# Layer 1 attention: packed products gathered in bursts every second step, maxima in whole rows over 41 steps a head, quads chained without a drain

## What is computed

```python
qkv = x @ w_qkv + b_qkv
q, k, v = jnp.split(qkv, 3, axis=-1)
q, k, v = (to_heads(q), to_heads(k), to_heads(v))
dots = jnp.einsum('bhid,bhjd->bhij', q, k) * scale
attn = jax.nn.softmax(dots, axis=-1)
out = jnp.einsum('bhij,bhjd->bhid', attn, v)
```

## Time and profile before

| | |
|---|---|
| median of 3 runs | 10340.24 us (10335.65 to 10344.37) |
| span of the profiled execution | 10375.5 us |
| mean granted TensorE clock | 0.809 |
| busy PE, DVE, ACT, GpSimd | 8825.9 (85%), 5783.3 (56%), 4145.5 (40%), 3261.0 us (31%) |
| layer 1 attention | about 3229 to 8560 us of the span |

### The profile page before, as it was taken

How to read it: one execution, slowest core, us unless ns; L and a number is a source line. 1 busy time by engine, 2 the same in 40 slices (tenths; PEclk the granted TensorE clock), 3 DMA queues, 4 the chain that set the end, 5 groups by cost and what they waited for, 6 DMA issues and landing times. The chain is left out here.

```text
span 10375.5 us, 158377 instructions
## 1 busy us (share of the span) xinstructions
PE 8825.9 (85%) x47072; PEld 4663.3 (45%) x47072; DVE 5783.3 (56%) x13683; ACT 4145.5 (40%) x9073; POOL 3261.0 (31%) x1854
## 2 busy tenths in 40 slices
PE   4499989997667999998999989999999885448888
PEld 3355545554444444444444444444444334325555
DVE  4355555555557976675766757766676004324444
ACT  1255555553000055555555555555555660001111
POOL 2000000000000055555555555555555670142211
PEclk8655555555876599999999999999999996569999
DMA  4511121101533001202112021111211004211110
GB/s 137 88 20 20 20 35 20 20 8 49 178 123 103 10 20 28 56 21 56 27 24 56 19 56 30 31 45 30 47 28 41 14 5 127 78 40 42 44 34 21
DMA packets 368839, 480.22 MB, mean 46 GB/s; under 512 B 154040, under 2 KB 322362, under 8 KB 354855
## 3 DMA queue, kind: packets, MB, share of 16 engines
q1 hardware_dynamic: 344551, 426.24, 17.0%
q0 software_dynamic: 23424, 43.45, 1.6%
HBM read 298.80 MB, written 180.34 MB: 46 GB/s over the span
## 5 line engine op out<-in xcount | busy, mean ns | idle before, releaser
L1057 POOL TENSOR_TENSOR a_added<-a_P 128x896 f32<-128x896 f32 x1344 | 2805.3, 2107 | 3517.1 <-ACT a_P L1029 3516.8
L935 DVE TENSOR_REDUCE a_tops<-a_ps 128x1 f32<-128x448 f32 x5600 | 3166.2, 632 | 1322.8 <-PE a_ps L843 1319.5
L1029 ACT ACTIVATE a_P<-a_ps 128x448 f32<-128x448 f32 (+1 forms) x5600 | 2610.3, 548 | 2600.3 <-PE a_ps L901 2599.3
L901 PE MATMUL a_ps<-a_qp,a_kp 98*128 98x448 f32 (+1 forms) x5600 | 1946.8, 399 | 171.4 <-DMA a_qp<-scratch_neg 97.9
L843 PE MATMUL a_ps<-a_hk,a_hq 96*128 96x448 f32 (+1 forms) x4900 | 1922.6, 406 | 118.9 <-DMA a_hk<-scratch_k 96.8
L843 PEld LDWEIGHTS a_ps<-a_hk,a_hq 96*128 96x128 f32 (+1 forms) x4900 | 917.7, 188 | 1205.3 <-DVE a_tops L935 1047.2
L901 PEld LDWEIGHTS a_ps<-a_qp,a_kp 98*128 98x128 f32 (+1 forms) x5600 | 1008.0, 189 | 951.7 <-ACT a_P L1029 637.8
L860 PE MATMUL a_ps<-a_P,a_vt 128*32 128x448 f32 (+1 forms) x11200 | 1362.2, 558 | 0.0
L459 DVE CUSTOM_DVE_ANT_0 n_sm<-n_ps,n_bias 112x448 f32<-112x448 f32 x928 | 578.1, 624 | 850.8 <-PE n_ps L390 850.8
L485 ACT ACTIVATE n_P<-n_sm,n_mx 112x448 f32<-112x448 f32 x928 | 620.2, 668 | 845.4 <-DVE n_mx L459 845.4
L400 PE MATMUL n_ps<-n_idn,n_P 112*112 112x112 f32 x3712 | 923.5, 404 | 21.5 <-DVE n_P L466 21.5
(11 more groups left out here) (174 smaller groups left out, 6476.7 us busy)
## 6 DMA issues: line engine op xcount, KB each, us to landing
a_qp<-scratch_q SPq DMA_DIRECT2D x168, 224.0 KB, 3.8
a_hq<-scratch_q SPq DMA_DIRECT2D x84, 392.0 KB, 7.3
a_hk<-scratch_k SPq DMA_DIRECT2D x84, 392.0 KB, 8.6
a_kp<-scratch_k SPq DMA_DIRECT2D x96, 320.0 KB, 4.9
scratch_t<-o_ts SPq DMA_DIRECT2D x8, 3136.0 KB, 13.2
e_w<-in_w SPq DMA_DIRECT2D x16, 1024.0 KB
p_xs<-in_x SPq DMA_DIRECT2D x4, 3136.0 KB, 15.3
scratch_v<-p_vs SPq DMA_DIRECT2D x4, 3136.0 KB, 12.5
```

What stands on the lines that cost most here:

```text
L901: pe.matmul(PS[0:rows_of(t), i_s % 3, 0:GW], kp[0:98, hh, 128 * t:128 * t + rows_of(t)], qp[0:98, hh, GW * j:GW * j + GW], start=True, sto ...
L935: dve.tensor_reduce(tops[0:rows_of(t), KT * hh + t, k:k + 1], PS[0:rows_of(t), MAX + i % MAXES, 0:GW], AX_X, ALU.max).then_inc(topped, 1)
L1029: act.activation(P[0:rows_of(t), (2 * n + pair) % (2 * RING), hh % 2, :], PS[0:rows_of(t), (4 * n + hh) % 3, 0:GW], ACT.Exp).then_inc(expe ...
L1057: pool.tensor_tensor(added2[:, a % 6, :, :], P[:, (2 * n + pair) % (2 * RING), :, :], P[:, (2 * n + 2 + pair) % (2 * RING), :, :], ALU.add ...
```

## The change

1. **Bursts.** Mixes and sums are issued only at the end of odd steps: `bursts()` gives each step a list, as a rule one sum and two mixes, in that order. A sum may follow its pair by three steps (`SUM_LAG`). The first mix of a column group doesn't stand directly behind another mix; then it moves to the next burst, which has three.
2. **Maxima.** A head has 41 steps. `maxima_by` now spreads 25 whole rows of seven products over 37 of them, and the products due are dealt out behind the four scores of a step. Maxima are negated at step 165, turned at 167, split at 168.
3. **No drain.** PE, DVE, ACT and GpSimd no longer wait at a quad's end. The last groups' mixes, sums, copies, reciprocals, division and store run on in the next quad's first steps. SP stores the negated maxima at step 169 and loads them for six of the seven column groups; the seventh, with its columns of `qp`, comes at step 0 of the next quad, the last key and value tiles at step 3. Each column group and each key group has its own semaphore, and PE waits for it where it is first used. Each engine's program now has the first quad, a loop of six and the last quad; before it was a loop of seven and the last (ACT, GpSimd: a loop of eight; GpSimd now one and a loop of seven).
4. The first quad's maxima use six banks in place of three.

```diff
         RING, MAXES = 5, 3
-        HEAD_STEPS = 42
+        HEAD_STEPS = 41
+        SUM_LAG = 3
         idn = sb("idn", [128, 128])
         ones = sb("ones", [128, HD])
...
+        NEG_AT, TURN_AT, SPLIT_AT = 4 * HEAD_STEPS + 1, 4 * HEAD_STEPS + 3, 4 * HEAD_STEPS + 4
...
         def maxima_by(n):
 
             hh = min(n // HEAD_STEPS, 3)
-            first, end = HEAD_STEPS * hh + 1, HEAD_STEPS * hh + HEAD_STEPS - 3
-            done = work(min(max(n, first), end)) - work(first)
-            return HMX * hh + HMX * done // (work(end) - work(first))
+            first, end = HEAD_STEPS * hh + 4, HEAD_STEPS * hh + HEAD_STEPS
+            done = min(max(n, first), end) - first
+            return HMX * hh + NG * (KT * done // (end - first))
...
+        def bursts():
+            out, mixes, sums = [], [], []
+            for n in range(2 * STEPS):
+                j, t = divmod(n % STEPS, KT)
+                mixes.append((n // STEPS, n % STEPS))
+                if t % 2 == 1:
+                    sums.append((n, (n // STEPS, j, t // 2)))
+                parts = []
+                if n % STEPS % 2 == 1:
+                    while sums and sums[0][0] <= n - SUM_LAG:
+                        parts.append(("sum",) + sums.pop(0)[1])
+                    while mixes and mixes[0][0] * STEPS + mixes[0][1] < n:
+                        if mixes[0][1] % KT == 0 and parts and parts[-1][0] == "mix":
+                            break
+                        parts.append(("mix",) + mixes.pop(0))
+                out.append(parts)
+            return out[:STEPS], out[STEPS:]
+        opening, steady = bursts()
+        tail = [part for parts in steady for part in parts if part[1] == 0]
+        carried = [[(part[0], part[1] - 1) + part[2:] for part in parts] for parts in steady]
...
+        TAKE_AT = [burst_of(lambda p: p[:3] == ("mix", 0, KT * j + KT - 1)) + 1 for j in range(NG)]
+        TAKE_SUMS_AT = [burst_of(lambda p: p[0] == "sum" and p[1:3] == (0, j) or p[:3] == ("mix", 0, KT * j + KT - 1)) + 1
+                        for j in range(NG)]
```

On SP, in `quad` (the first hunk is at the start of its loop over the steps, the second at the end of it; `store_neg` is the first half of the old `move_neg`, `load_neg` its second):

```diff
-                for n in range(STEPS + 1):
+                for n in range(STEPS):
+                    if not first:
+                        if n == 0:
+                            sp.wait_ge(scored, q * HS)
+                            sp.sem_inc(steps, 1)
+                            load_neg_tail(q)
+                            load_q(q, NG - 1)
+                        if n == 3:
+                            sp.wait_ge(mixed, q * STEPS)
+                            sp.sem_inc(steps, 1)
+                            load_kv(q, len(KGROUPS) - 1)
+                        if n == 12:
+                            sp.wait_ge(divided, q * NG)
+                            sp.sem_inc(steps, 1)
+                            sp.dma_start(S["y1T"][q - 1, :, GW * (NG - 1):N], yo[:, (NG - 1) % 2, :])\
...
+                    if more and n >= STEPS - KT + 8 and n % 5 == 3:
+                        done = n - 3
+                        sp.wait_ge(mixed, q * STEPS + done)
+                        sp.sem_inc(steps, 1)
+                        load_kv(m, (done - (STEPS - KT)) // 5 - 1)
+                    if more and n == SPLIT_AT + 1:
+                        store_neg(m)
+                        load_neg(m)
```

On PE:

```diff
+            def burst(q, parts):
+                for part in parts:
+                    if part[0] == "mix":
+                        mix(q + part[1], part[2])
+                    else:
+                        sum_pair(q + part[1], part[2], part[3])
...
+            def quad(q, first, more):
                 m = q + 1
-                pe.wait_ge(loaded, m * (16 * LOADS))
                 pe.wait_ge(neg_loaded, m * 16)
...
+                for n in range(STEPS):
+                    j, t = divmod(n, KT)
+                    if t == 0:
+                        pe.wait_ge(q_loaded[j], m * 48)
+                        if j == NG - 1:
+                            pe.wait_ge(neg_tail_loaded, m * 16)
+                    if j == 0 and t % 5 == 0:
+                        pe.wait_ge(kv_loaded[t // 5], m * KV_LOADS[t // 5])
+                    due = maxima_by(n + 1) if more else 0
...
+                    for hh in range(4):
+                        i_s = 4 * n + hh
...
+                        until = i + (due - i + 3 - hh) // (4 - hh)
                         while i < until:
-                            product_for_maximum(m, i, lambda hh: hq, lambda hh: hk)
+                            product_for_maximum(m, i, lambda hh: hq, lambda hh: hk, MAX, MAXES)
                             i += 1
-                    if more and n == STEPS - 5:
+                    burst(q, opening[n] if first else carried[n])
+                    if more and n == TURN_AT:
                         assert i == MX
                         turn_maxima(m)
-                pe.wait_ge(taken, m * NG)
-                pe.wait_ge(sums_taken, m * NG)
+                if not more:
+                    burst(q, tail)
```

On ACT, at the head of each step:

```diff
+            def quad(q, first, more):
                 for n in range(STEPS):
                     t = n % KT
+                    for j in range(NG):
+                        if TAKE_AT[j] == n:
+                            take(q, j)
+                        if TAKE_AT[j] == n + STEPS and not first:
+                            take(q - 1, j)
+                        if TAKE_SUMS_AT[j] == n:
+                            take_sums(q, j)
+                        if TAKE_SUMS_AT[j] == n + STEPS and not first:
+                            take_sums(q - 1, j)
                     for hh in range(4):
```

More of the change, by code:

```diff
@@ new lines, in layer1_attend @@
+        opening, steady = bursts()
+        tail = [part for parts in steady for part in parts if part[1] == 0]
+        carried = [[(part[0], part[1] - 1) + part[2:] for part in parts] for parts in steady]
+        order = []
+        for parts in opening + steady:
+            for part in parts:
+                if part[0] == "sum":
+                    order.append(part[1:])
+                elif part[2] % KT == KT - 1:
+                    order.append((part[1], part[2] // KT, PAIRS))
+        own = [(j, u) for quad, j, u in order if quad == 0]
@@ L760, in layer1_attend, with since @@
+        def since(eng, semaphore, q, each, k):
+            if not isinstance(q, int) or q * each + k > 0:
+                eng.wait_ge(semaphore, q * each + k)
         block = ctx.enter_context(nc.Block())
@@ L876, in sum_pair @@
                                      added2[:, (2 * (PAIRS * j + u) + hh // 2) % 6, hh % 2, :],
-                                     start=(u == 0), stop=(u == PAIRS - 1))
+                                     start=(u == 0), stop=SUM_NUMBER[j, u] == LAST_SUM[j])
                 last.then_inc(summed, 1)
-            def quad(q, more):
+            def burst(q, parts):
+                for part in parts:
+                    if part[0] == "mix":
+                        mix(q + part[1], part[2])
+                    else:
+                        sum_pair(q + part[1], part[2], part[3])
@@ L925, in _, with maximum @@
             turn_maxima(0)
-            with pe.Fori(0, QUADS - 1) as q:
-                quad(q, True)
-            quad(QUADS - 1, False)
+            quad(0, True, True)
+            with pe.Fori(1, QUADS - 1) as q:
+                quad(q, False, True)
+            quad(QUADS - 1, False, False)
         @block.vector
         def _(dve):
-            def maximum(m, i):
+            def maximum(m, i, bank, banks):
                 hh, t, k = i // HMX, i // NG % KT, i % NG
                 dve.wait_ge(keyed, m * MX + i + 1)
-                dve.tensor_reduce(tops[0:rows_of(t), KT * hh + t, k:k + 1], PS[0:rows_of(t), MAX + i % MAXES, 0:GW],
+                dve.tensor_reduce(tops[0:rows_of(t), KT * hh + t, k:k + 1], PS[0:rows_of(t), bank + i % banks, 0:GW],
@@ L961, in divide, with quad @@
                 dve.wait_ge(taken, q * NG + j + 1)
-                if j >= 2:
-                    dve.wait_ge(stored[j % 2], q * (16 * ((NG + 1 - j % 2) // 2)) + 16 * (j // 2))
+                since(dve, stored[j % 2], q, 16 * ((NG + 1 - j % 2) // 2), 16 * (j // 2))
                 dve.wait_ge(inverted, q * (4 * NG) + 4 * (j + 1))
                 dve.tensor_tensor(yo[:, j % 2, :], y[:, j % 2, :], sums[:, :], ALU.mult).then_inc(divided, 1)
-            def quad(q, more):
+            def quad(q, first, more):
                 m = q + 1
```

227 lines of the change are left out of this document (114 added, 113 removed).

## The result

The changed kernel takes 10757.77 us (10745.82 to 10762.47) against 10340.24: ratio 1.0404, 95% interval 1.0385 to 1.0422. The forecast was 10650, range 10360 to 10860. Span of its profiled execution 10760.6, clock 0.817.

A forecast was written before the change was run, and what follows sets the result against it. PE was taken to bound the kernel before; after, DVE holds the (7, 7) pairs. Seven quads +273, head loads +15 and last quad +22 make +310 on the median of 10340: 10650 us, range 10360 to 10860.

The forecast's parts named there:

- Pair prices: Times worked out for two-step pairs by maxima products per step: 9.56, 7.28, 7.05 and 5.79 us, exact to some 0.1.
- (0, 0): Pair of steps without maxima products: forecast 5.79 us, against 5.54 in the kernel before.
- (7, 7): Pair with seven maxima products in each step: held by DVE's 14 reductions, 7.5 us, forecast 9.56 us.
- Bursts on PE: Gathered packed groups remove two of three round trips between widths per pair, 0.31 each, so PE's work falls 0.62 us.
- some 4 us a quad: Cost of reciprocals, 0.83 us each on DVE, that fall at the middle of (7, 7) pairs.
- the clock rival: PE's waits between bursts without maxima lower the clock, one burst in six at half clock: +235, so 10885 us; 12%.
- The seam at nothing: Quad boundary: negated maxima stored six steps ahead cover 12.1 us, so costed at nothing; up to 12 a quad if failing.
- the extra code at 25: One more unrolled quad copy for PE, DVE, ACT and SP: at most 25 us at two seams, taken as nothing.
- Head loads at +15: Waits for loads at each quad's first head, 2 us each, +15 us in all; other heads' waits go.
- (7, 0): Pair with seven maxima products in the first step and none in the second: forecast 7.05 us.
- (0, 7): Pair with no maxima products in the first step and seven in the second: forecast 7.28 us.
- The banks hide it: Rival: ACT and DVE keep ahead, PE stays the bound, (7, 7) under about 7.5 us, total 9755 us; 18%.

The follow-up runs named there:

- the third run: The changed kernel without bursts (mix and due sum end each step) and with maxima products dealt out one by one: 10136.47 us, ratio 0.9805 to the kernel before.

## Why the prediction was right, point by point

- **Pair prices.** Worked out 9.56, 7.28, 7.05 and 5.79; measured 9.50, 7.32, 7.10 and 5.64 (medians at full clock). In the last quad (0, 0) took 5.73, near the 5.79, but partly by luck: 0.1 of it is ACT's later start in straight code, which the sum didn't know of. The claim that DVE's reductions hold (7, 7) was shown by halving them (7.41), the claim that rows of seven are the loss by undoing that line alone (415 us). This step, the (7, 7) pair held by DVE, decides the sign and nearly all of the size.
- **Bursts on PE.** 0.62 a pair less work for PE than the kernel before, by 0.31 for each round trip between the widths. This is worked out, not measured by itself. Against one packed part at each step one change is saved, and with DVE out of the way 0.22 of it shows. What I had not said clearly is that even with single products bursts would lose to no bursts, by 2%.
- **The step that was mis-sized: "some 4 us a quad" for reciprocals.** The place was right, between the 7s of a pair, but there are six such places a quad, and their cost isn't 0.7 but 2.1 us on average, because the clock falls at 35 of them; where it doesn't, the pair takes 10.2, 0.7 more. That is 12.8 us a quad instead of 4, 62 us more than the sum had. This is the mechanism of the clock rival, which I had put in the last quad and the steps without maxima; there it made 8 of 87 pairs and 15 of 91 longer (seven of these at a quad's start). A rival put in the wrong place was worth about half of its 235 us.
- **The seam at nothing.** Cover for the negated maxima held: no wait. But the seam isn't free: steps 174, 0 and 1 take 13.9 us on average where the sum has 3 x 2.895 = 8.7, so 5.3 a quad, 37 in all. Where it comes from is read off the seams: some 4 us without a semaphore at five of them, and half clock behind all seven. I had bounded the extra code at 25, for the two seams between copies, and taken nothing; those two show no such stop, the loop's five do.
- **Head loads at +15.** Too high: 0.4 us in all. Nothing waited for the first head's loads, with four DMAs ahead of them.
- **Smaller.** (7, 0) is 0.1 higher on average, since ACT's copy stands ahead of the exponentials at a group's start (7.9 at steps 24 and 74), 24 us. (0, 7) makes 9 more, (0, 0) apart from the seam 7, (7, 7) without a reciprocal 12 less. Last quad +31 instead of +22, with eight pairs that have a stretch at half clock; 4 of these 9 are the last seam's. First maxima as before, as forecast. Together with the -15: 62 + 37 + 24 + 9 + 7 - 12 + 5 - 15 = 117, against 429 - 310 = 119 by which attention grew more than forecast in the traces. The medians differ by 418 and so miss the forecast by 108; the 11 us between are outside attention or spread.
- **The rivals.** "The banks hide it" was to show a (7, 7) under 7.5 us; it took 9.5. With reductions at half cost it does come to 7.4, so the rival was right on what the pair would take, but not on the total: 10099 us, not 9755. The rule on draining in the Trainium skill (TensorEngine Tiling, Key Properties) holds in the rows (0.31 us for a round trip between the widths), but alone it would have given the wrong sign here; the Trainium skill's one on PSUM evacuation (same page, PSUM Bottleneck) fits what was measured, 9.50 against 7.41 for a (7, 7) pair when the reductions take half the columns.

Left open: what of the dealing in the third run (no products behind packed parts, sum ahead of mix, one step less of lag) makes its pair 0.29 cheaper than that of the chained kernel with the old dealing; these were not tried one by one. A fourth difference is in the traces: inside a head a step there gets 3, 4 or 6 products, in the third run 4 or 5. A step with a sum takes 4.48 with six and 3.97 with five. Nor was a version of PE's program without a loop tried, which would show whether the stop of 4 us is the loop's.

## What to carry to other kernels

Before gathering one engine's expensive switches into a burst, ask how long the engines it feeds can live on what is buffered: here three banks are 1.6 us of DVE's work and a burst is 2.4. Ask also whether PE's waits between bursts let the clock fall. And deal out work for a slower engine in pieces no larger than its buffers, from the first slot of a step: one line that rounds to rows of seven cost 4%, one product moved ahead of the scores gained 1.4%. The best version found, 0.9647 of the kernel before, keeps the chained quads and drops bursts and rows.

## What the runs showed of the hardware that was not expected

- In a stretch where PE's weight loads wait 0.2 to 0.5 us for DVE again and again, one wait of 0.76 us more was followed by a fall of the granted clock to 1.2 GHz in 35 of 41 cases, while the same stretch without it stayed at 2.4 (0 of 141). Issuing products twice kept it at 2.4 (0 of 182), and so did dropping the bursts (none at the 41 places).
- ACT's first exponential of a step starts 0.51 us behind its score inside a loop and 0.59 in straight code, here in both quads outside the loop; 13 us over 175 steps.
- Where PE's loop goes round there is a stop of some 4 us that no semaphore explains (five of five seams), and none where straight code goes on into another copy (0 of 2).
